# Last stage of a vision-tower kernel on one Trainium2 core: layer statistics in narrow matmuls, two broadcasts from a row, and a new table of places

## The chip, the cores and the metric

One NeuronCore of a Trainium2 chip runs the whole program in one launch. The metric is the device time of one execution in microseconds (us), the median of several; lower is better.

## The reference, cut to what matters

A tokenizer of two attention stages and a strided 3x3 unfold with a projection gives h: 4 images, 3136 tokens each, 768 channels, float32. The last stage of the kernel computes that projection and one layer on h:

```python
h = h + _L0_attn_ref(_layernorm(h), A, W_B, b_B, W_C, b_C, W_D, b_D, p_Delta)
h = h + _L0_ffn_ref(_layernorm(h), enc_w, enc_b, sw_w, sw_b, w1, b1, w2, b2)

def _ssm_forward(x, A, W_B, b_B, W_C, b_C, W_D, b_D, p_Delta):
    Bproj = x @ W_B + b_B                                   # 16 columns
    Cproj = x @ W_C + b_C
    delta = jax.nn.softplus(x @ W_D + b_D + p_Delta)        # W_D has one column
    dA = delta[..., None] * A
    A_bar = jnp.exp(dA)
    B_bar = (A_bar - A) / dA * delta[..., None] * Bproj[:, :, None, :]
    # h = a * h + b * x over the tokens, y = sum over the 16 states of c * h

# ffn: x_enc = x @ enc_w + enc_b (64 columns), 8 experts by argmax of a softmax,
#      gelu(x @ w1[e] + b1) @ w2[e] + b2, times the largest probability
```

## The kernel before

**Stages.** Two performer stages fill the first 3.1 ms or so and are not touched. The function `tail` is the last stage. It works in 28 units (4 images of 7 strips) of T = 448 tokens, channels on partitions in 6 chunks of 128. A unit has 24 steps (6 chunks by 4 groups of states); one step scans 4 x 448 columns.

**A step** on its engines: GpSimd (POOL) multiplies x by B into a ring of six buffers (`weigh_in`, L1604). ScalarE (ACT) writes four decays into PSUM (L1886), in two pairs, each as soon as VectorE has scanned that pair of the step before. VectorE (DVE) weighs each pair (L1995, two instructions) and scans it (L2004). ACT keeps the last states (`keep_states`, L1847). POOL multiplies by C (`weigh_out`, L1616), two steps behind its `weigh_in`. TensorE (PE) sums the states in four matmuls of 32 output rows (L1697) into PSUM bank 4 (YB); after four steps it adds h (L1701), and ACT copies the bank back to h (`add_to_h`, L1875).

**Other work** is put between the steps of unit i: `front(i + 1, k)` prepares the next unit (projection by six matmuls, "taps", a chunk, L1656 and L1658, and its copy to h, L1812; squares, L1804; sums, B, C, z and delta), and `mlp(i - 1, k)` finishes the last one (second layer norm, encoding, experts, routing, masks, output in eight blocks, L1759 to L1762). Each engine runs its program strictly in order, and the step k at which a piece stands on each engine is a constant of a table written by hand: P_ for PE, A_ for ACT, V_ for DVE.

```python
P_PJ, P_MU, P_VAR, P_Z, P_BC = 1, 7, (8, 10), 11, 9
A_HW, A_MU, A_SQ, A_RS, A_MX, A_SP = 5, 11, (9, 13), 14, (16, 17), (17, 18)
```

All this work shares the three PSUM banks BS, BX and BF (5, 6, 7): every tap goes to BF, so the tap of a chunk waits until ACT has copied the one before. Sums over the channels are matmuls with a 128 x 128 matrix of 1/768, whose answer stands in all 128 rows; W_D is repeated to 128 columns (`wz`) for the same reason.

**ACT's order in a step:** `add_to_h` where due, `start_states` (L1857), four decays, `keep_states` of the step before, then mlp and front. A wait in these stands ahead of the next decays. SyncE (SP) issues the loads, stores and spreads of x and delta through DRAM in program order too.

## Time and profile before

| | us |
|---|---|
| median of 3 runs (8669.71 to 8670.3) | 8670.22 |
| the profiled execution | 8669.5 |
| its span, first to last instruction | 8667.7 |
| PE busy | 7500.9 (87%) |
| DVE busy | 6217.8 (72%) |
| POOL busy | 5557.6 (64%) |
| ACT busy | 4309.3 (50%) |
| mean granted clock of PE | 0.916 |

The span is from the first instruction to the last. Busy shares are over the whole program; the last stage begins at about 3.1 ms, and what limits it is read from its own stretches. A matmul in float32 shows as two rows, so "x12" is six matmuls. Idle time is given in brackets with the instruction that ended it.

### The profile page before, as it was taken

Reading aid. Unit: us, or ns where it says so; the run is one execution under the profiler, and the core shown is the slowest. Engines: PE = TensorE matmul, PEld = TensorE weight load, DVE = VectorE, ACT = ScalarE, POOL = GpSimd, SP = SyncE. Lnnn points to the kernel's source line nnn. Section 1 sums busy time; section 2 is a strip of 40 time slices with the busy share of each in tenths; the row PEclk is TensorE's granted clock in tenths of the full one; section 3 lists DMA queues with packets and bytes.
Section 4 is the critical chain, followed back from the end, with each engine's and each line's share of the span. In section 5 each row is a group of like instructions: output and inputs, shape, how many; then the busy total and the mean of one; then the engine's idle time right before and its main releaser. Section 6 shows DMA issues by size and latency. Waiting matters only on the chain.

```text
span 8667.7 us, 87075 instructions
## 1 busy us (share of the span) xinstructions
PE 7500.9 (87%) x31228; PEld 3123.7 (36%) x31228; DVE 6217.8 (72%) x6601; ACT 4309.3 (50%) x7753; POOL 5557.6 (64%) x2486
## 2 busy tenths in 40 slices
PE   8999999979999856888888888878888888788877
PEld 6444444334444312333333333333333333333333
DVE  2566666822333339888888888888888888888884
ACT  3666666833444425455445444554444445544442
POOL 0111111267666319888888888888888888888884
PEclk9999999989999977988889999888989998899888
DMA  1111111145545222232333322323333233233321
GB/s 38 40 42 45 42 46 36 50 100 110 102 101 104 58 85 88 98 124 99 108 118 116 104 96 99 126 96 113 114 114 104 96 109 115 96 121 107 114 102 52
DMA packets 356921, 786.65 MB, mean 91 GB/s; under 512 B 70437, under 2 KB 282870, under 8 KB 349000
## 3 DMA queue, kind: packets, MB, share of 16 engines
q1 hardware_dynamic: 320440, 690.78, 26.3%
q0 software_dynamic: 21712, 51.75, 2.4%
q10 hardware_dynamic: 14336, 38.54, 1.2%
q8 instruction: 247, 4.05, 0.2%
q14 instruction: 186, 1.52, 0.1%
HBM read 597.39 MB, written 183.35 MB: 90 GB/s over the span
## 4 chain that ended last, share of the span: by engine, by line
PE 36%; DVE 16%; ACT 6%; issue 6%; POOL 0%; DMA 0%; SPq 0%; DVEq 0%; ACTq 0%; POOLq 0%
PE ps L1651 7%; DVE v L2004 7%; PE ps L1759 7%; DVE v L1995 6%; PE ps L1658 6%; PE ps L1656 6%; PE ps L1697 3%; ACT ps L1886 3%; PE ps L1647 2%; PE ps L1760 2%; PE ps L1762 2%; PE ps L1701 1%; DVE dl L1985 1%; DVE gm L2081 1%; ACT gm L1911 1%
## 5 line engine op out<-in xcount | busy, mean ns | idle before, releaser
L1616 POOL TENSOR_TENSOR v<-v,ct 128x1792 f32<-128x1792 f32 x672 | 2257.7, 3360 | 859.1 <-ACT st L1847 858.5
L2004 DVE TENSOR_TENSOR_SCAN v<-ps,v 128x901 f32<-128x901 f32 x1344 | 2732.2, 2033 | 92.2
L1886 ACT ACTIVATE ps<-dr,aa 128x448 f32<-128x448 f32 x2688 | 1586.0, 627 | 1526.2 <-DVE v L2004 1508.8
L1604 POOL TENSOR_TENSOR v<-xr,bt 128x1792 f32<-128x1792 f32 x672 | 2257.9, 3360 | 97.5 <-DMA xr<-h_by_channel 97.5
L1995 DVE SCALAR_TENSOR_TENSOR v<-ps,aa,v 128x448 f32<-128x448 f32 x2688 | 1689.1, 670 | 547.6 <-ACT ps L1886 528.9
L236 POOL DMA_DIRECT2D tokens<-ob x448 | 235.3, 532 | 1529.6 <-DVE ob L563 1486.7
L1759 PE MATMUL ps<-w_or_w,gm 128*112 128x384 f32 x1792 | 728.4, 556 | 370.7 <-DVE gm L2081 278.1
L1697 PE MATMUL ps<-v,dg 128*32 128x448 f32 x5376 | 702.6, 597 | 196.6 <-ACT h L1875 120.1
L1759 PEld LDWEIGHTS ps<-w_or_w,gm 128*112 128x112 f32 x1792 | 337.3, 199 | 772.1 <-DVE gm L2081 320.5
L1651 PE MATMUL ps<-h,w_or_w 128*128 128x448 f32 x1344 | 537.4, 550 | 17.7 <-DVE gm L2048 17.7
L1812 ACT ACTIVATE h<-ps,pbias 128x448 f32<-128x448 f32 x168 | 106.3, 633 | 721.9 <-PE ps L1658 721.9
L1656 PE MATMUL ps<-x,wpa 128*128 128x448 f32 x1008 | 445.9, 577 | 17.7 <-ACT h L1812 10.7
L1658 PE MATMUL ps<-x,wpb 64*128 64x448 f32 x1008 | 447.8, 575 | 0.0
L929 PE MATMUL ps<-xt,wa 128*64 128x448 f32 x2016 | 435.1, 565 | 0.0
L552 DVE COPY ht<-ps 112x512 f32<-112x512 f32 x112 | 77.4, 691 | 464.8 <-ACT kp L433 464.8
L1647 PE MATMUL ps<-sq,jm 128*128 128x448 f32 x672 | 317.3, 613 | 60.5 <-ACT ot L1920 56.5
L1651 PEld LDWEIGHTS ps<-h,w_or_w 128*128 128x128 f32 x1344 | 250.5, 191 | 300.5 <-issue 279.7
L586 DVE RECIPROCAL qpn<-qpn 128x448 f32<-128x448 f32 x112 | 330.7, 2953 | 3.9
L1697 PEld LDWEIGHTS ps<-v,dg 128*32 128x32 f32 x5376 | 110.1, 112 | 600.1 <-issue 292.1
L1746 PE MATMUL ps<-wpb 9*128 9x448 f32 x224 | 152.1, 769 | 194.7 <-DVE gm L2081 194.0
L1238 DVE TENSOR_TENSOR kq<-ps,rsa 128x896 f32<-128x896 f32 x56 | 61.1, 1092 | 358.6 <-PE ps L937 337.6
L1651 PE MATMUL ps<-h,wz 128*128 128x448 f32 x336 | 192.4, 742 | 100.9 <-ACT rs L1824 100.9
(324 smaller groups left out, 11785.1 us busy)
## 6 DMA issues: line engine op xcount, KB each, us to landing
xr<-h_by_channel SPq DMA_DIRECT2D x168, 896.0 KB, 7.5
dr<-delta_by_channel SPq DMA_DIRECT2D x168, 896.0 KB, 6.1
x<-tokens SPq DMA_DIRECT2D x252, 224.0 KB, 5.3
tokens<-ob POOLq DMA_DIRECT2D x448, 112.0 KB, 2.4
w_or_w<-in_w SPq DMA_DIRECT2D x29, 1536.0 KB, 6.4
w_or_w<-centred_w SPq DMA_DIRECT2D x27, 1536.0 KB, 6.4
h_by_channel<-h SPq DMA_DIRECT2D x112, 336.0 KB, 10.8
delta_by_channel<-dl SPq DMA_DIRECT2D x112, 336.0 KB, 5.1
```

The source lines that it names most:

```text
L929: mm(ps[half[g], o, 0:T], wa[:, j, cols], xt[:, 2 * (n % 3) + g, 0:TR2, j:j + 2 * S2 - 1:2], start=(j == 0), stop=False)
L1604: tt(v[:, n % RING, :, 2:T + 2], xr[:, dc % 2, :].rearrange("p (i t) -> p i t", i=4), bt[:, q:q + 1, :].to_broadcast([128, 4, T]), ALU.mul ...
L1616: tt(v[:, n % RING, :, 2:T + 2], v[:, n % RING, :, 2:T + 2], ct[:, q:q + 1, :].to_broadcast([128, 4, T]), ALU.mult).then_inc(s_cm, 1)
L1647: mm(into, jm[:, :], sq[:, dc % 3, :], start=(dc == 0), stop=(dc == DC - 1)).then_inc(s_var[ln], 1)
L1651: last = mm(into, weights(dc), h[:, i % 3, dc, :], start=(dc == 0), stop=(dc == DC - 1))
L1656: mm(into, even(j), x3[:, 0:TR3, j:j + 2 * S3 - 1:2], start=(j == 0), stop=False)
L1658: last = mm(into, odd(j), x3[0:64, 1:TR3 + 1, j:j + 2 * S3 - 1:2], start=False, stop=(j == 2))
L1697: last = mm(ps[32 * g:32 * g + 32, YB, 0:T], dg[:, 4 * k + g, :], v[:, n % RING, g, 2:T + 2], start=(q == 0), stop=False)
L1759: mm(into[:, 0:D // 2], gm[:, m, cs], w2[:, m, lo:lo + D // 2], start=(m == 0), stop=False)
L1886: fn(decay(g), dr[:, dc % 2, g, :], ACT.Exp, scale=aa[:, 4 * k + g:4 * k + g + 1]).then_inc(s_a, 1)
L1995: stt(row, decay(g), aa[:, 4 * k + g:4 * k + g + 1], row, ALU.subtract, ALU.mult).then_inc(s_wt, 1)
L2004: nc.vector.tensor_tensor_scan(row, flat[:, 1024 * pair + 1:1024 * pair + GW + T + 2], row, 0.0, ALU.mult, ALU.add).then_inc(s_sc, 1)
```

## The change

- **LN 1 (`sums_1`).** For each chunk three matmuls stand in a row: B, C and W_D together (49 output rows from partition 0), one tap of the token means (9 rows from 64) and the sum of squares (32 rows from 96), all into bank BS. Before, squares (128 rows, BF), B and C (48 rows, BS), means (BF) and W_D repeated (128 rows, BF) were four sets of six.
- **LN 2 (`sums_2`).** For each chunk the encoding (64 rows from 64), the mean (32 rows from 0) and the squares (32 rows from 32) go to bank BX.
- **z and deviation from a row.** z is scaled with C in one DVE instruction, and one matmul with `pick` spreads its row over 128 partitions. The second variance is subtracted in 32 rows and spread in the same way. The DVE scaling of z (L1970) is gone; ACT takes the logarithm of the first variance twice, in 32 rows each.
- **Banks.** The taps of chunks 0, 2, 5 go to BF, those of 1, 3, 4 to BS; the four expert products to BF, BF, BX, BS.
- **ACT** does its other work in half steps: `step` is cut in two pairs, work of place k stands between them and work of place k + 0.5 behind. `keep_states` now stands ahead of the second pair.
- **SP** stores and spreads delta in two halves, and four of its places move.
- **Places.** Nearly every constant of the table is new; TAIL is 29.

```diff
-        P_PJ, P_MU, P_VAR, P_Z, P_BC = 1, 7, (8, 10), 11, 9
-        A_HW, A_MU, A_SQ, A_RS, A_MX, A_SP = 5, 11, (9, 13), 14, (16, 17), (17, 18)
-        V_Z, V_BC, V_DL = 15, 14, (18, 19)
-        P_SQ, P_MEAN, P_ENC, P_IN, P_LOG, P_TURN = (0, 2), 1, 4, 5, 6, 10
-        P_MASK, P_OUT = (12, 13, 14, 15), (16, 17, 18, 18, 19, 20, 21, 22)
-        A_SQ2, A_MS, A_RS2, A_EX, A_GL = (2, 4), 5, 7, 11, 14
-        A_OUT = (21, 22, 23, 23, 24, 25, 26, 27)
-        V_VAR, V_ENC, V_IN, V_LOG, V_EQ, V_OH, V_MASK = 6, 8, 9, 10, 12, 14, (16, 17, 18, 19)
+        P_PJ, P_SUM, P_Z = (1, 3, 4, 5, 7, 8), (9, 11), 14
+        A_HW, A_SQ, A_MU, A_RS = (5, 6.5, 8, 9, 10.5, 12), (9.5, 12.5), 15, 14.5
+        A_MX, A_SP = (17, 17.5), ((18, 18.5), (19, 19.5))
+        V_BC, V_DL = 15, (18, 19)
+        P_SUM2, P_VAR, P_IN, P_LOG, P_TURN = (2, 4), 6, (10, 12, 13, 14), 8, 11
+        P_MASK, P_OUT = (15, 15, 17, 17), (18, 19, 20, 20, 21, 22, 23, 24)
+        A_SQ2, A_MS, A_RS2, A_EX, A_GL = (1, 5.5), 8, 9.5, 12, 17
+        A_OUT = (22, 22.5, 23.5, 24, 25, 26, 27, 28)
+        V_VAR, V_ENC, V_IN, V_LOG, V_EQ, V_OH, V_MASK = 7, 9, (12, 14, 15, 16), 11, 12, 13, (17, 17, 18, 18)
...
+            def sums_1(i, chunks):
+                for dc in chunks:
+                    pe.wait_ge(s_sq[0], DC * i + dc + 1)
+                    mm(ps[0:49, BS, 0:T], wbc[:, dc, :], h[:, i % 3, dc, :], start=(dc == 0), stop=(dc == DC - 1))
+                    tap(ps[few, BS, 0:T], lambda j: wma[:, j, :], lambda j: wmb[:, j, :], dc)
+                    mm(ps[top, BS, 0:T], jm[:, 0:32], sq[:, dc % 3, :], start=(dc == 0),
+                       stop=(dc == DC - 1)).then_inc(s_var[0], 1)
...
+                    if dc == 1:
+                        after(pe, s_oa, 2 * NCH * (i - 2))
+                        after(pe, s_bcs, 2 * i)
+                    if dc >= 2:
+                        pe.wait_ge(s_hw, DC * i + (dc - 1 if dc < 4 else 4))
...
+                if k == P_Z:
+                    pe.wait_ge(s_bcs, 2 * (i + 1))
...
+                    mm(bank(BF), pick[mid, 0, :], bcs[mid, :], start=True, stop=True).then_inc(s_z, 1)
...
+                    if m == 3:
+                        pe.wait_ge(s_bcs, 2 * min(i + 3, UNITS))
+                        pe.wait_ge(s_mu, min(i + 3, UNITS))
...
                     if i < UNITS:
                         start_states(i, k)
-                        step(i, k)
+                        step(i, k, 0)
+                    if i >= 1 and k == 2:
+                        add_to_h(i - 1, DC - 1)
+                    if i < UNITS and k >= 6 and k % 4 == 2:
+                        add_to_h(i, k // 4 - 1)
+                    others_due(i, k)
                     if i >= 1 and k == 0:
                         keep_states(i - 1, STEPS - 1)
                     elif i < UNITS and k > 0:
                         keep_states(i, k - 1)
...
+                    if i < UNITS:
+                        step(i, k, 1)
+                    others_due(i, k + 0.5)
```

**What it moves on the engines.** PE, steps 5 and 6 of a unit in the middle, before (dg is the sum of the states, w_or_w an expert product, wpa and wpb the taps):

```order
L1697 MATMUL ps<-v,dg 32x448 x4
L1651 MATMUL ps<-h,w_or_w 128x448 x6
L1656 MATMUL ps<-x,wpa 128x448 x3
L1658 MATMUL ps<-x,wpb 128x448 x3
L1697 MATMUL ps<-v,dg 32x448 x4
L1651 MATMUL ps<-h,w_or_w 128x448 x6
L1728 MATMUL ps<-wpb 112x8 x4
L1656 MATMUL ps<-x,wpa 128x448 x3
L1658 MATMUL ps<-x,wpb 128x448 x3
```

Now, PE's steps 5, 6 and the start of 7:

```order
L1734 MATMUL ps<-v,dg 32x448 x4
L1670 MATMUL ps<-x,wpa 128x448 x3
L1672 MATMUL ps<-x,wpb 128x448 x3
L1734 MATMUL ps<-v,dg 32x448 x4
L1749 MATMUL ps<-rs2t,pick 128x448
L1734 MATMUL ps<-v,dg 32x448 x4
L1738 MATMUL ps<-h,ident 128x448
L1670 MATMUL ps<-x,wpa 128x448 x3
L1672 MATMUL ps<-x,wpb 128x448 x3
```

The expert products have left these steps for 10 to 14, the next tap stands two steps on, and step 6 holds only the spread of the second variance.

PE, the sums of the first layer norm, before, from step 8 on:

```order
L1697 MATMUL ps<-v,dg 32x448 x4
L1651 MATMUL ps<-h,w_or_w 128x448 x6
L1647 MATMUL ps<-sq,jm 128x448 x3
L1697 MATMUL ps<-v,dg 32x448 x4
L1651 MATMUL ps<-h,wbc 48x448 x6
L1697 MATMUL ps<-v,dg 32x448 x4
L1733 MATMUL ps<-ident,eq 9x112 x4
L1647 MATMUL ps<-sq,jm 128x448 x3
L1697 MATMUL ps<-v,dg 32x448 x4
L1701 MATMUL ps<-h,ident 128x448
L1651 MATMUL ps<-h,wz 128x448 x6
```

Now, the start of step 9; the three narrow matmuls come three times here and three times in step 11:

```order
L1734 MATMUL ps<-v,dg 32x448 x4
L1679 MATMUL ps<-h,wbc 49x448
L1670 MATMUL ps<-x,wma 9x448
L1681 MATMUL ps<-sq,jm 32x448
L1679 MATMUL ps<-h,wbc 49x448
```

ACT, step 9 before (v<-st starts the states, ps<-dr,aa are decays, h<-ps,pbias is the copy of a tap):

```order
L1857 ACTIVATE v<-st 128x4
L1886 ACTIVATE ps<-dr,aa 128x448 x4
L1847 ACTIVATE st<-v 128x4
L1812 ACTIVATE h<-ps,pbias 128x448
L1804 ACTIVATE sq<-h 128x448 x3
```

Now, its step 9 with the half step behind it:

```order
L1899 ACTIVATE v<-st 128x4
L1928 ACTIVATE ps<-dr,aa 128x448 x2
L1852 ACTIVATE h<-ps,pbias 128x448
L1889 ACTIVATE st<-v 128x4
L1928 ACTIVATE ps<-dr,aa 128x448 x2
L1943 ACTIVATE rs2t<-ps,small 128x448
L1945 ACTIVATE rs2t<-rs2t 128x448
L1843 ACTIVATE sq<-h 128x448 x3
```

The copy of the tap and the kept states stand between the two pairs of decays; the statistics of the second layer norm and the squares stand behind the second pair.

## Rows read from the trace of the kernel before

**Rows 1.** Busy time by stretch: 20 units, units 1 to 26, unit 0, unit 27, the end
```profile
core 0: us, PE busy (x) PEld busy (x) DVE busy (x) ACT busy (x) POOL busy (x), PEclk, DMA share, GB/s
3967.50:7808.30 3840.80, 3234.19 (x11217) 1288.95 (x11216) 3357.50 (x3481) 1871.17 (x3980) 3199.75 (x961) 0.90 0.32 108
3395.50:8384.90 4989.40, 4189.11 (x14500) 1667.87 (x14496) 4364.65 (x4525) 2430.71 (x5170) 4159.99 (x1249) 0.89 0.32 108
3218.40:3395.50 177.10, 91.01 (x314) 27.66 (x314) 160.08 (x155) 82.32 (x175) 161.15 (x49) 0.71 0.34 115
8384.90:8562.30 177.40, 121.37 (x428) 46.90 (x424) 161.78 (x165) 76.46 (x172) 154.44 (x47) 0.76 0.19 72
8562.30:8667.70 105.40, 95.12 (x327) 45.63 (x326) 8.30 (x20) 16.72 (x30) 3.36 (x1) 0.95 0.15 50
```

**Rows 2.** Waits in the 20 units: us in total, times, longest us
```profile
DVE v L1995 <- ACT ps L1886: 402.0, 126, 4.8
DVE ps L1976 <- ACT rs L1826: 8.3, 20, 0.4
...
ACT h L1812 <- PE ps L1658: 527.5, 112, 7.5
ACT h L1875 <- PE ps L1701: 235.7, 80, 7.6
...
POOL v L1616 <- ACT st L1847: 640.5, 350, 5.3
```

**Rows 3.** Timeline of PE, steps 5 and 6 of unit 4: start, us
```profile
4029.79 0.96 PE L1697 MATMUL ps<-v,dg 128*32 128x448 f32 x8
4030.68 4.78 PE L1651 MATMUL ps<-h,w_or_w 128*128 128x448 f32 x12
4035.30 2.56 PE L1656 MATMUL ps<-x,wpa 128*128 128x448 f32 x6
4040.38 0.96 PE L1697 MATMUL ps<-v,dg 128*32 128x448 f32 x8
```

**Rows 4.** Timeline of ACT and DVE, the same place
```profile
4036.43 2.03 DVE L2004 TENSOR_TENSOR_SCAN v<-ps,v 128x901 f32<-128x901 f32 x1
...
4040.49 0.63 ACT L1812 ACTIVATE h<-ps,pbias 128x448 f32<-128x448 f32 x1 [7.53 <-PE ps L1658]
...
4043.79 1.27 DVE L1995 SCALAR_TENSOR_TENSOR v<-ps,aa,v 128x448 f32<-128x448 f32 x2 [4.81 <-ACT ps L1886]
```

**Rows 5.** Timeline of PE in the second performer stage
```profile
2502.06 0.96 PE L932 MATMUL ps<-x,wc 128*64 128x448 f32 x4
2502.86 2.55 PE L929 MATMUL ps<-xt,wa 128*64 128x448 f32 x12
2505.24 0.96 PE L932 MATMUL ps<-x,wc 128*64 128x448 f32 x4
2506.14 1.02 PE L937 MATMUL ps<-x,wc 64*64 64x448 f32 x8
```

**Rows 6.** Groups of ACT and DVE in the 20 units: busy us, mean ns
```profile
L1970 DVE TENSOR_TENSOR ps<-ps,rs 128x448 f32<-128x448 f32 x20 | 12.1, 606 | 0.0
...
L1832 ACT ACTIVATE dl<-ps,pc 128x448 f32<-128x448 f32 x120 | 66.4, 620 | 0.0
...
L1911 ACT ACTIVATE gm<-gm,b 128x448 f32<-128x448 f32 x80 | 47.0, 657 | 0.2
L1911 ACT ACT_TABLE_LOAD x20 | 25.7, 1283 | 0.4
```

**Rows 7.** Timeline of PE after a wait in unit 14
```profile
6010.42 7.57 PE L1651 MATMUL ps<-h,wz 128*128 128x448 f32 x12 [3.83 <-ACT rs L1824]
```

**Rows 8.** Timeline, from the first tap to the first decays
```profile
3142.13 4.18 PE L1656 MATMUL ps<-x,wpa 128*128 128x448 f32 x6 [6.99 <-DVE w_or_w L2114]
...
3198.84 4.78 PE L1651 MATMUL ps<-h,wz 128*128 128x448 f32 x12 [0.72 <-ACT rs L1824]
...
3214.96 3.76 SPq L1488 DMA_DIRECT2D delta_by_channel<-dl  x4
...
3229.94 2.31 ACT L1886 ACTIVATE ps<-dr,aa 128x448 f32<-128x448 f32 x4 [16.87 <-DMA dr<-delta_by_channel]
```

**Rows 9.** Timeline of PE behind the last scan
```profile
8583.06 2.52 PE L1647 MATMUL ps<-sq,jm 128*128 128x448 f32 x6 [1.01 <-ACT ot L1920]
...
8596.93 4.78 PE L1651 MATMUL ps<-h,w_or_w 128*128 128x448 f32 x12
```

**Rows 10.** DMA issues in the 20 units: KB each, median us to landing
```profile
xr<-h_by_channel SPq DMA_DIRECT2D x120, 896.0 KB, 7.6
...
w_or_w<-in_w SPq DMA_DIRECT2D x20, 1536.0 KB, 6.4
```

More of the change, by code:

```diff
@@ L1555, in _ @@
                 spread_c(0, q)
-            store_delta(0)
-            spread(0, 0)
+            spread_x(0, 0)
+            store_delta(0, 0)
+            spread_delta(0, 0)
+            store_delta(0, 1)
             for i in range(UNITS):
@@ L1642, in _ @@
             mm = nc.tensor.matmul
-            def squares_sum(i, ln, into, chunks):
-                for dc in chunks:
-                    pe.wait_ge(s_sq[ln], DC * i + dc + 1)
-                    mm(into, jm[:, :], sq[:, dc % 3, :], start=(dc == 0), stop=(dc == DC - 1)).then_inc(s_var[ln], 1)
             def over_chunks(into, weights, i):
@@ L1652, in over_chunks, with tap, sums_2 @@
                 return last
-            def taps(into, even, odd):
-                for j in range(3):
+            def tap(into, even, odd, j):
+                if j < 3:
                     mm(into, even(j), x3[:, 0:TR3, j:j + 2 * S3 - 1:2], start=(j == 0), stop=False)
-                for j in range(3):
-                    last = mm(into, odd(j), x3[0:64, 1:TR3 + 1, j:j + 2 * S3 - 1:2], start=False, stop=(j == 2))
-                last.then_inc(s_pj, 1)
+                else:
+                    return mm(into, odd(j - 3), x3[0:64, 1:TR3 + 1, j - 3:j - 4 + 2 * S3:2], start=False,
+                              stop=(j == 5))
+            def sums_1(i, chunks):
[5 more added lines that the diff above has]
+                       stop=(dc == DC - 1)).then_inc(s_var[0], 1)
+            def sums_2(i, chunks):
+                for dc in chunks:
+                    pe.wait_ge(s_sq[1], DC * i + dc + 1)
+                    mm(ps[up, BX, 0:T], enc[:, dc, :], h[:, i % 3, dc, :], start=(dc == 0), stop=(dc == DC - 1))
+                    mm(ps[low, BX, 0:T], jm[:, 0:32], h[:, i % 3, dc, :], start=(dc == 0), stop=(dc == DC - 1))
+                    mm(ps[mid, BX, 0:T], jm[:, 0:32], sq[:, dc % 3, :], start=(dc == 0),
+                       stop=(dc == DC - 1)).then_inc(s_var[1], 1)
             def front(i, k):
-                if P_PJ <= k < P_PJ + DC:
-                    dc = k - P_PJ
+                for dc in range(DC):
+                    if P_PJ[dc] != k:
+                        continue
                     cols = slice(128 * dc, 128 * dc + 128)
@@ L1820, in front @@
                     squares(i, 0, range(3, DC))
+                if k == A_MU:
+                    act.wait_ge(s_var[0], DC * (i + 1))
+                    fn(means(i), ps[few, BS, 0:T], ACT.Identity, bias=mub[few, :]).then_inc(s_mu, 1)
                 if k == A_RS:
@@ L1875, in add_to_h, with step @@
                 fn(h[:, i % 3, dc, :], bank(YB), ACT.Copy).then_inc(s_hy, 1)
-            def step(i, k):
+            def step(i, k, pair):
                 dc, q = divmod(k, Q)
                 n = STEPS * i + k
-                if q == 0:
+                if q == 0 and pair == 0:
                     act.wait_ge(s_dr[dc % 2], 16 * ((DC // 2) * i + dc // 2 + 1))
-                for g in range(4):
-                    if g % 2 == 0 and n > 0:
-                        free_pair(n - 1, g // 2)
+                if n > 0:
+                    free_pair(n - 1, pair)
+                for g in range(2 * pair, 2 * pair + 2):
                     fn(decay(g), dr[:, dc % 2, g, :], ACT.Exp,
@@ L1925, in mlp, with others_due @@
                         act.dma_start(dst, ot[:, ch % 2, :]).then_inc(s_out[ch % 2], 16)
+            def others_due(i, k):
+                if i >= 2 and k + STEPS < TAIL:
+                    mlp(i - 2, k + STEPS)
+                if i >= 1:
+                    mlp(i - 1, k)
+                if i + 1 < UNITS:
+                    front(i + 1, k)
             act.sem_inc(s_in, 1)
```

245 lines of the change are left out of this document (118 added, 127 removed).

## The prediction

> **What bounds the kernel now.** I read the busy time by stretch first. Twenty units of the last stage take 3840.8 us, 192.0 each; DVE is busy for 167.9 of a unit, PE for 161.7, POOL for 160.0 [rows 1]. Three engines stand near 85% and none is full, so the waits come next. In these 20 units DVE waits 402.0 us for ACT's decays and 8.3 for the deviation, 20.5 a unit, and for nothing else that is listed [rows 2]. ACT is not slow (1871 of 3841 us busy [rows 1]): it stands 527.5 us before its copies of the taps and 235.7 before its copies of h, both times for PE, and its program is in order, so the next decays stand behind that copy. POOL waits only for the states that ACT keeps, 640.5 us [rows 2]. The timeline shows one case: PE's step 5 holds the sum of the states, an expert product and a tap and takes from 4029.79 to 4040.38, 10.6 us [rows 3]. ACT waits 7.53 us for this tap, and DVE, whose last scan began at 4036.43, gets its decays at 4043.79, 4.81 us late [rows 4]. A mean step of DVE without its waits is (192.0 - 20.5) / 24 = 7.15 us. So PE binds the kernel in the steps where taps and other products stand together, and DVE elsewhere.
>
> From rows 3, each start taken to the next: the sum of the states costs 0.89 us, six matmuls of a set 4.62 (0.77 each), a tap set 5.08 (0.85 each). I write Tk for the end of DVE's step k. PE can begin step k when POOL has weighed it, some 3.7 us behind Tk (3.36 of POOL and a kept state).
>
> **PE's load.** Removed are 36 matmuls of sets of six (12 squares, W_D, B and C, mean, encoding) and 6 taps of the means: 36 x 0.77 + 6 x 0.85 = 32.8 us a unit. Added are 12 groups of three and two spreads (2 x 0.77 = 1.5). The trace holds no group of unlike widths. The lower end is the group of four equal 32-row matmuls, 0.89, which gives 10.7; the upper is every matmul for itself with a break before it. The nearest row for the break: four rows of 128x64 followed by the same shape start 0.80 us before it, followed by 64x64 they start 0.90 before it [rows 5], so 0.10 a change, and 36 x 0.87 = 31.3. I take the value between: only equal shapes run together, which are the means with the squares in three groups and the two 32-row sums in six, so 9 x 2 + 3 x 3 = 27 turns of 0.87, 23.5 us, because the only change of shape in the rows does show a break. PE then has 161.7 - 32.8 + 23.5 + 1.5 = 153.9 us a unit (141.1 at the lower end).
>
> The Trainium skill speaks against the change here: "TensorEngine Tiling (Array Packing)", Tiling Modes, says that changing the tiling mode, not just the tile, drains TensorE. The break in rows 5 agrees in kind; no row shows unlike shapes side by side. By that rule the groups cost the 23.5 us of the sum, and without it 10.7.
>
> **Where PE's work stands.** Before, its steps 1 to 8 held eight states (7.1), six tap sets and that of the means (7 x 5.1), the squares of both norms by halves (4.6), mean, encoding and four experts (27.7) and 2.6 of small work: 77.7 us, 9.7 a step against 7.15. Now steps 1 to 8 hold eight states, six taps, six groups (10.4), a spread and the same small work: about 51 us, 6.4 a step. The heaviest are 4 (0.9 + 5.2 + 5.1 = 11.2) and 11 (10.5, odd taps), each with a light neighbour. The experts stand in 10, 12, 13, 14, with 5.5 each.
>
> Then the copies, step by step. A tap's copy on ACT, between the pairs of step k, comes about 2 us before T(k-1). Tap 0 (PE 1) ends at T2 + 3.5 and is copied near T4 - 2, 8 us of slack; tap 4 (PE 7) ends near T8 + 4.4 and its copy at 10.5 is due at T9 + 1.4, 4 us; tap 5 (PE 8), behind a wait for the encoding at T9 + 0.7, ends near T10 and is due near T11 - 2. The second bank is what lets PE run ahead. Copies of h moved one step earlier, from 7 to between the pairs of 6; PE's output blocks moved from two in 18 to two in 20, so that the block of h in step 19 no longer stands behind them. The 20.5 us of DVE's waiting go, and 0.6 of the removed scaling of z (L1970) [rows 6]: 192.0 - 20.5 - 0.6 = 170.9 us a unit, the floor.
>
> **What comes in its place.** (a) Expert 1 (PE 12) stands behind the long step 11, whose turn of the routing waits for DVE until T12 + 2, and ends at about T14: DVE waits 0.8 us. (b) Expert 3 (PE 14) now waits for B and C, which DVE writes 2.6 us behind T15. PE idles some 3.5 us there. After 3.83 us of idling a set took 7.57 instead of 4.78 us [rows 7]; with the same surcharge the product ends 1 us behind T16, 1.0 us of DVE. Behind this wait on PE stand the spread of z and the states of step 15; both are wanted later. (c) ACT's place 17 holds between the pairs two table loads, four gelus and three copies of z, 2 x 1.28 + 4 x 0.66 + 3 x 0.62 = 7.1 us [rows 6], while from its start to the moment DVE wants the second pair there are about 4.8 us: 2.3 us. Together 4.1, so **175.0 us a unit**. The two logarithms of 32 rows, the copy of the means and the deviation lie in ACT's idle time, which is half of it; if a wait falls into the same half step they cost their own 0.6 us. `keep_states` now stands ahead of the second pair, delays it by 0.2 us of 2 us of slack and serves POOL a microsecond earlier. DVE's narrow operations keep their durations.
>
> SP: the w2 load waits for expert 3 (PE 14, about T16), and behind it in the queue stands the spread of x for the last chunk, which POOL wants near T17 + 4. The load takes 6.4 us and a spread 7.6 to land [rows 10], so POOL may idle up to 4 us; it has 175.0 - 160.0 = 15 us to spare, so it costs nothing here (a rival below). Delta's two stores give the next unit's first spread some 5 us earlier; it had slack.
>
> **The ends.** Units 1 to 26 took 4989.4 us [rows 1], now 26 x 175.0 = 4550.0: 439.4 saved. Unit 0 saves the 0.6 of z. Unit 27 has no front: 177.4 us with DVE busy 161.8 [rows 1]; with the same 3.6 us of small gaps as a full unit (171.5 - 167.9) and 1.3 of waits it is 166.7, 10.7 saved. From the first tap to the first decays 87.8 us pass [rows 8]. There each removed set of six is on the path; 18 squares, B and C and W_D plus the means' taps (19.0) become 13.8 of groups and one spread, the taps no longer wait for each copy (5 x 0.7), and delta is stored in halves: about 15 (10 to 22). Behind the last scan the squares, the mean and the encoding take 13.9 us on PE (8583.06 to 8596.93) [rows 9] and become 10.4, output blocks lag by less, a longer chain to the first expert costs some back: 8 (3 to 12).
>
> **Sum.** 439.4 + 0.6 + 10.7 + 15 + 8 = 473.7. Against the profiled execution's 8669.5 us that is **8196 us**; the median of the runs is 0.7 above it, which changes nothing.
>
> **The rivals.**
> 1. *PE still binds part of the unit.* At 153.9 us of 175 it is as full as before (84% then, 88% now) and has four waits of its own (encoding, routing, B and C, output copies). If each of the turns cost the upper 31.3 us instead of 23.5, PE needs 162 us; with the waits a unit is about 182: 8669.5 - 26 x 9.9 - 34 = 8378. For it: no row shows unlike shapes together. Against it: the load is spread evenly.
> 2. *POOL starves behind the w2 load.* The late spread of x and states kept behind ACT's longer middle part take POOL's reserve; a unit of 178 gives 8669.5 - 26 x 13.9 - 34 = 8274.
> 3. *The clock falls, and the kernel becomes slower.* PE's granted clock is 0.90 with PE busy 84% of the time, 0.76 with 68% (unit 27) and 0.71 with 51% (unit 0) [rows 1]. The sets at the prices of rows 3 add up to 142 us a unit at full speed. If the thinned work left the clock at 0.70, PE would need 142 / 0.70 = 203 us, 11 more than now: 8669.5 + 26 x 11 - 34 = 8922. It decides from 142 / 192 = 0.74 down. Against it: PE stays above 80% busy, between the first two stretches, so I expect 0.87 or more. "TensorE: Matmul & The Clock Gate", Part 1, of the Trainium skill holds that half rate is the default and that activity releases it, which is this rival's rule; the three stretches agree with it in direction.
> 4. *The change doesn't do what it says.* ACT's waits on PE are only hidden waits on something else in the ring, and DVE loses the same 20 us behind another releaser: within 0.2%, about 8660.
>
> **Chances.** The forecast 0.64 (own range 8090 to 8250: with the lower price of the groups and no new waits 171 us a unit, 8092; with 177, 8248), rival 1 0.16, rival 2 0.12, rival 3 0.04, rival 4 0.04. A measurement tells about 0.2%, 17 us, from no change. Faster by more 0.92, within 0.04, slower 0.04. The range of 8 in 10 runs from 8090 to 8380 and takes in rivals 1 and 2.
>
> **What would show it.** A full unit of 175 us, with DVE above 95% busy; DVE's wait for decays under 5 us a unit instead of 20.1, and most of it at the gelus; ACT's waits for taps and h nearly gone (38 us a unit now); POOL at about 92%; PE 150 us or less a unit and its clock not under 0.85. In the groups, starts of the three matmuls within 0.02 us of each other would mean 0.89 a group; 0.4 us apart would mean turns. I am wrong if DVE still waits over 10 us a unit, if its waits name POOL's `v`, or if the granted clock of a unit is under 0.8.

## The result and the profile after

| | us |
|---|---|
| median of 4 runs (8262.34 to 8265.36) | 8263.43 |
| kernel before, same chip (8669.5 to 8670.3) | 8669.97 |
| ratio, 95% interval | 0.9531 [0.9515, 0.9548] |
| the profiled execution | 8263.1 |
| its span, first to last instruction | 8261.3 |
| mean granted clock of PE | 0.918 |

The changed kernel takes 4.7% less time. The profiled executions differ by 406.4 us; 473.7 were predicted. Busy time by stretch in the changed kernel; the stretches are unit 0, units 1 to 26, the same 20 units as in [rows 1], unit 27, and the end behind the last scan:

```profile
core 0: us, PE busy (x) PEld busy (x) DVE busy (x) ACT busy (x) POOL busy (x), PEclk, DMA share, GB/s
3208.00:3385.10 177.10, 88.51 (x304) 23.21 (x304) 159.44 (x154) 82.97 (x176) 162.16 (x49) 0.68 0.36 117
3385.10:7988.40 4603.30, 4030.82 (x14295) 1492.07 (x14296) 4354.56 (x4499) 2456.79 (x5197) 4149.57 (x1249) 0.90 0.36 117
3915.10:7457.50 3542.40, 3107.15 (x11036) 1151.68 (x11034) 3349.69 (x3461) 1890.84 (x4000) 3192.01 (x961) 0.90 0.36 117
7988.40:8156.80 168.40, 118.60 (x437) 42.80 (x436) 161.73 (x164) 77.01 (x171) 153.55 (x47) 0.78 0.21 76
8156.80:8261.30 104.50, 91.92 (x314) 42.89 (x312) 8.29 (x20) 16.82 (x30) 3.35 (x1) 0.92 0.15 50
```

Against [rows 1], units 1 to 26 gained 4989.4 - 4603.3 = 386.1 us, unit 27 9.0, the end 0.9 and the time up to unit 0 10.4 (it begins at 3208.0 instead of 3218.4); unit 0 gained nothing. That is the whole 406.4. A full unit takes 3542.4 / 20 = 177.1 us instead of 192.0, with DVE busy 94.6% of it. PE's busy time fell by 6.3 us a unit (161.7 to 155.4) while the unit fell by 14.9.

The waits in the 20 units (us in total, times, longest), of DVE and the longest of ACT:

```profile
DVE gm L2121 <- PE ps L1785: 51.1, 40, 2.0
DVE v L2038 <- ACT ps L1928: 39.7, 20, 2.0
DVE gm L2090 <- PE ps L1665: 24.7, 37, 1.2
...
ACT ps L1928 <- DVE v L2047: 935.7, 400, 6.3
```

L1928 are the decays, L2038 and L2047 DVE's weighing and scan, L1665 an expert product, L1785 an expert's mask, L2121 DVE's product with it, L2090 DVE's scaling of an expert product. DVE's 402.0 us behind the decays [rows 2] are 39.7, one wait a unit. ACT no longer waits for PE before its copies of taps or of h at all; PE holds it for 23.2 us before the first variance, and otherwise it waits for DVE. New are 51.1 us before the masks, 2.6 a unit, and 24.7 before the scaling of expert products, 1.2 a unit.

What makes DVE wait there can be followed in the timeline of unit 14 (start and duration in us, in brackets the idle time before and its releaser). ACT, its place 17 (L1952 the gelus, L1873 the copies of z, L1889 the kept state):

```profile
5804.63 1.28 ACT L1952 ACT_TABLE_LOAD   x1
5805.93 2.35 ACT L1952 ACTIVATE gm<-gm,b 128x448 f32<-128x448 f32 x4
5808.29 1.28 ACT L1953 ACT_TABLE_LOAD   x1
5809.59 1.68 ACT L1873 ACTIVATE dl<-ps,pc 128x448 f32<-128x448 f32 x3
5811.15 0.21 ACT L1889 ACTIVATE st<-v 128x4 f32<-128x4 f32 x1
```

POOL's weighing of the finished states, PE's sum of the states (L1734) and masks, and DVE:

```profile
5811.44 3.36 POOL L1634 TENSOR_TENSOR v<-v,ct 128x1792 f32<-128x1792 f32 x1 [6.97 <-ACT st L1889]
...
5815.74 1.72 PE L1734 MATMUL ps<-v,dg 128*32 128x448 f32 x8 [4.79 <-ACT h L1917]
5821.50 1.72 PE L1734 MATMUL ps<-v,dg 128*32 128x448 f32 x8 [4.03 <-POOL v L1634]
5823.15 3.35 PE L1785 MATMUL ps<-wpb 9*128 9x448 f32 x4
...
5812.48 1.28 DVE L2038 SCALAR_TENSOR_TENSOR v<-ps,aa,v 128x448 f32<-128x448 f32 x2 [2.03 <-ACT ps L1928]
5825.12 0.62 DVE L2121 TENSOR_TENSOR gm<-gm,ps 128x448 f32<-128x448 f32 x1 [1.69 <-PE ps L1785]
```

One block of ACT makes both waits. Its second pair of decays comes 2.03 us late, and the states of step 16, which it keeps just ahead of that pair, come so late that POOL stands 6.97 us. From there POOL works without a gap and is through with step 17 at 5821.44 only. PE's sum of that step waits for it until 5821.50; behind it stand two masks, and after the idle time sum and masks take twice as long as in steps without a wait, the level of 1.2 instead of 2.4 GHz: 1.72 us for the sum instead of 0.96, and 3.35 for the masks instead of the 1.76 of the two at 5809.19. The granted clock of that stretch, 5821.5 to 5826.5, is 0.50. With 0.89 for the sum and 0.88 for each mask both would have been there at about 5824.2, and DVE was free at 5823.43: an estimate of some 0.2 us of waiting instead of 2.56. So the late states cost that much because the idle time that they make is also followed by the lower level.

### The profile page after: what moved, and what is told of

Same layout as the page of the kernel before. It is cut to its first block, busy times and chain, and to the rows that moved or that the text cites. A ratio compares the mean times of both kernels' runs of the same rounds, so it can differ in the third digit from the quotient of the medians.

```text
span 8261.3 us, 86870 instructions
## 1 busy us (share of the span) xinstructions
PE 7327.8 (89%) x31004; PEld 2931.6 (35%) x31004; DVE 6205.4 (75%) x6573; ACT 4337.3 (53%) x7781; POOL 5547.7 (67%) x2487
## 4 chain that ended last, share of the span: by engine, by line
DVE 28%; PE 15%; issue 11%; POOL 4%; ACT 4%; DMA 0%; DVEq 0%; SPq 0%; ACTq 0%; POOLq 0%
DVE v L2038 13%; DVE v L2047 13%; PE ps L1665 3%; POOL v L1634 3%; PE ps L1670 2%; PE ps L1672 2%; PE ps L1734 2%; PE ps L1679 2%; POOL v L1622 1%; DVE dl L2028 1%; PE ps L1681 1%; PE ps L1785 1%; ACT ps L1928 1%; ACT gm L1952 1%; PE ps L1798 0%
## 5 line engine op out<-in xcount | busy, mean ns | idle before, releaser
L2047 DVE TENSOR_TENSOR_SCAN v<-ps,v 128x901 f32<-128x901 f32 x1344 | 2732.1, 2033 | 95.0 <-DVE v L2038 2.7
L1928 ACT ACTIVATE ps<-dr,aa 128x448 f32<-128x448 f32 x2688 | 1595.9, 626 | 1319.6 <-DVE v L2047 1303.2
L2038 DVE SCALAR_TENSOR_TENSOR v<-ps,aa,v 128x448 f32<-128x448 f32 x2688 | 1687.5, 669 | 71.5 <-ACT ps L1928 67.9
L1734 PE MATMUL ps<-v,dg 128*32 128x448 f32 x5376 | 792.3, 632 | 616.2 <-POOL v L1634 395.1
L1798 PE MATMUL ps<-w_or_w,gm 128*112 128x384 f32 x1792 | 694.4, 535 | 3.0 <-DMA w_or_w<-in_w 3.0
L1665 PE MATMUL ps<-h,w_or_w 128*128 128x448 f32 x1344 | 588.7, 592 | 84.9 <-DVE bcs L2022 84.9
L1889 ACT ACTIVATE st<-v 128x4 f32<-128x4 f32 x672 | 140.9, 210 | 893.5 <-DVE v L2047 893.5
L1670 PE MATMUL ps<-x,wpa 128*128 128x448 f32 x1008 | 497.1, 632 | 7.6 <-DVE w_or_w L2154 6.9
L1734 PEld LDWEIGHTS ps<-v,dg 128*32 128x32 f32 x5376 | 126.3, 114 | 1026.3 <-POOL v L1634 550.2
L1672 PE MATMUL ps<-x,wpb 64*128 64x448 f32 x1008 | 452.2, 580 | 0.0
L1665 PEld LDWEIGHTS ps<-h,w_or_w 128*128 128x128 f32 x1344 | 268.4, 206 | 408.3 <-issue 302.6
L1670 PEld LDWEIGHTS ps<-x,wpa 128*128 128x128 f32 x1008 | 202.0, 210 | 260.3 <-issue 257.8
L290 PE MATMUL ps<-wki,h 128*112 128x256 f32 x896 | 275.9, 389 | 1.9 <-DVE hu L544 1.9
L1672 PEld LDWEIGHTS ps<-x,wpb 64*128 64x128 f32 x1008 | 175.8, 187 | 275.1 <-issue 275.1
```

The costliest lines, as they stand in the source:

```text
L1665: last = mm(into, weights(dc), h[:, i % 3, dc, :], start=(dc == 0), stop=(dc == DC - 1))
L1670: mm(into, even(j), x3[:, 0:TR3, j:j + 2 * S3 - 1:2], start=(j == 0), stop=False)
L1672: return mm(into, odd(j - 3), x3[0:64, 1:TR3 + 1, j - 3:j - 4 + 2 * S3:2], start=False, stop=(j == 5))
L1734: last = mm(ps[32 * g:32 * g + 32, YB, 0:T], dg[:, 4 * k + g, :], v[:, n % RING, g, 2:T + 2], start=(q == 0), stop=False)
L1798: mm(into[:, 0:D // 2], gm[:, m, cs], w2[:, m, lo:lo + D // 2], start=(m == 0), stop=False)
L1928: fn(decay(g), dr[:, dc % 2, g, :], ACT.Exp, scale=aa[:, 4 * k + g:4 * k + g + 1]).then_inc(s_a, 1)
```

## The experiments

All but the three that say so go from the changed kernel. They ran on chips on which the kernel before takes 8677 to 8678 us; by its ratio the changed kernel would take 0.9531 x 8678 = 8271 there (an estimate), and it is the ratios that are compared. A unit is the mean over 20 full units of the profiled execution.

### The masks, the copies of z, and both

```diff
-        P_MASK, P_OUT = (15, 15, 17, 17), (18, 19, 20, 20, 21, 22, 23, 24)
+        P_MASK, P_OUT = (15, 15, 16, 16), (18, 19, 20, 20, 21, 22, 23, 24)
```

> Edit to the changed kernel: the third and fourth mask product of the experts move from PE's step 17 to its step 16, so they no longer stand behind the sum of the states of step 17, which POOL weighs late because ACT's block at place 17 keeps the states late. Theory A (place 17 is the cause of the masks' wait): DVE's 2.6 us a unit on the masks (L2121) go, a unit 177.1 becomes 174.5, time about 8263 - 27 x 2.6 = 8195. Rival B (the wait moves on: the next thing that is late is DVE's decays in the same step, so DVE waits the same time at L2038): a unit stays within 0.5 us of 177.1, time 8250 to 8263.

```diff
-        A_MX, A_SP = (17, 17.5), ((18, 18.5), (19, 19.5))
+        A_MX, A_SP = (17.5, 18), ((18, 18.5), (19, 19.5))
```

> Edit to the changed kernel: ACT's three capped copies of z (first half) move from the middle of place 17, where they stand behind the four gelus and two table loads, to half a step later, and the second half from there to 18. Theory A: the block before the second decay pair of step 17 shrinks from 7.1 to about 5.2 us, DVE's wait for decays (2.0 us a unit) goes, states are kept 1.9 us earlier and the masks' wait falls too: a unit 173 to 175, 8155 to 8215. Rival B (ACT's block isn't what ends last; the gelus must wait for DVE's last product anyway, and the copies of z now delay the first pair of step 18): DVE waits 2 us at another decay, a unit stays at 177, 8255 to 8270.

> Both edits (masks in PE's step 16, copies of z half a step later). If the two waits are separate costs, 2.6 + 2.0 us a unit go: a unit 172.5, 8263 - 27 x 4.6 = 8139. If both come from the one block of place 17, this gives no more than the better of the two single edits (about 8195).

Masks alone: 8184.91 us, ratio 0.9433 [0.942, 0.9446], a unit 174.0. Copies alone: 8243.26, 0.95 [0.9487, 0.9513], a unit 176.3. Both: 8144.18, 0.9386 [0.9374, 0.9399], a unit 172.5. DVE's waits in 20 units, for the three in this order:

```profile
DVE v L2038 <- ACT ps L1928: 40.5, 20, 2.0
DVE gm L2090 <- PE ps L1665: 17.1, 28, 0.8
```
```profile
DVE gm L2121 <- PE ps L1785: 66.3, 40, 2.8
...
DVE v L2038 <- ACT ps L1928: 8.1, 18, 0.5
```
```profile
DVE gm L2090 <- PE ps L1665: 19.1, 29, 1.2
DVE v L2038 <- ACT ps L1928: 8.1, 18, 0.5
```

With the masks in step 16 the wait for them is gone and nothing takes its place; the unit falls by 3.1 us, 0.5 more than that wait, of which 0.4 is a shorter wait at the experts. With the copies moved, the wait for decays falls from 2.0 to 0.4 us a unit, but the masks' wait grows from 2.6 to 3.3, so that only 0.8 of the 1.6 us reach the unit: that part of theory A fell. The reason is the next block. ACT's place 18 now holds the second three copies and the exponential, and keeps the states of step 17 behind them, so that POOL waits for just these. Its row in that run:

```profile
5811.67 3.36 POOL L1634 TENSOR_TENSOR v<-v,ct 128x1792 f32<-128x1792 f32 x1 [0.73 <-ACT st L1889]
```

Together the two edits give what the two waits promise, 4.6 us a unit. By ratio that is 0.0145, a little more than 0.0098 and 0.0031 of the single ones. The rival, that with one block behind both waits the two edits give no more than the better one, fell: the block is one, but it reaches DVE by two paths, and each edit opens one of them. This version beats both kernels and computes the same outputs.

### PE's load: the kernel before with less of it

These three go from the kernel before, and leave all places as they were.

```diff
-                    over_chunks(bank(BX), lambda dc: jm[:, :], i).then_inc(s_mean, 1)
+                    over_chunks(bank(BX), lambda dc: jm[:, :], i, DC - 1).then_inc(s_mean, 1)
...
```

> Edit to the kernel before: the mean, the product of W_D, that of B and C, and the encoding use one matmul instead of six each (the sixth chunk alone; five sixths of each sum are left out), 20 matmuls less, 15.4 us of PE a unit (161.7 to 146), everything in its old place. Theory L (load): PE has as much room as in the changed kernel, and the 20.5 us of waits for decays go: a unit under 177, about 8280 or less. Theory P (places): most of the wait stays, because in steps 1 to 6 ACT still wants each tap in the step in which PE makes it; the lighter steps are 4 (mean and encoding) and 9 to 11. A unit of 182 to 188, 8400 to 8570.

The next took the same number of matmuls from other steps, and the one after it took both (both edits in one kernel):

```diff
-                    over_chunks(bank(BS), lambda dc: w1[:, dc, 128 * m:128 * m + 128], i).then_inc(s_hm, 1)
+                    over_chunks(bank(BS), lambda dc: w1[:, dc, 128 * m:128 * m + 128], i, DC - 1).then_inc(s_hm, 1)
```

> Edit to the kernel before: each of the four expert products in PE's steps 5 to 8 uses one matmul instead of six (the sixth chunk alone; five sixths of each product are left out): 20 matmuls less, as many as in the run that thinned the mean, W_D, B and C and the encoding, which brought a unit from 192.0 to 187.7 us. Theory S (what counts is PE's load in the steps where one bank passes from tap to copy to tap: steps 5 and 6 hold a tap and an expert each, and step 7 the means' taps and an expert): the waits for decays of DVE's steps 9 to 12, 13.6 us a unit, go, and the wait of step 23 stays: a unit of 178 to 180, about 8300 to 8370. Theory L (any 15 us less of PE count the same): 187 to 188 a unit, about 8545.

> Edit to the kernel before: both cuts together, 40 matmuls less (five sixths of the mean, W_D, B and C, encoding and expert sums are left out), PE's load some 31 us a unit lower, all places as before. Theory S: the waits of steps 3, 9 to 12 go, and 4 us of step 23 stay, where ACT's copy of h stands behind two output products on PE: a unit of 176 to 178, 8260 to 8320. Rival (ACT's order alone makes part of the waits, whatever PE does): 182 or more, 8400 or above.

| | ratio to before | unit, us | PE busy a unit |
|---|---|---|---|
| kernel before | 1 | 192.0 | 161.7 |
| thin sums | 0.9846 [0.9833, 0.986] | 187.7 | 149.9 |
| thin experts | 0.9743 [0.9728, 0.9757] | 184.4 | 149.8 |
| both | 0.9732 [0.9717, 0.9746] | 184.4 | 138.5 |
| the change | 0.9531 [0.9515, 0.9548] | 177.1 | 155.4 |

This is the main finding, and none of the theories had it whole. The thin sums met theory P (182 to 188 us a unit), the thin experts fell between S and L, and both cuts together met the number of the rival, 182 or more. The place of the load counts: 20 matmuls out of the steps 5 to 8 give 7.6 us a unit, 20 out of others 4.3. But with 40 out and PE 17 us less busy than in the changed kernel, the unit is still 7.3 us longer than there. DVE still waits 12.6 us a unit for decays (20.1 before):

```profile
DVE v L1995 <- ACT ps L1886: 252.6, 60, 7.5
```

They stand at two places. One is in the middle of the unit, 6.9 us of the 12.6 (137.7 in 20 units), and its cause is new. PE's waits for DVE's scaling of an expert product show what came up. They add up to 45.0 us with thin sums and 98.8 with thin experts; the rows of the kernel before and of both cuts, in 20 units:

```profile
PE ps L1651 <- DVE gm L2048: 11.1, 20, 0.6
```
```profile
PE ps L1651 <- DVE gm L2048: 171.4, 51, 5.5
```

The timeline of the run with both cuts: PE's step 6, then ACT, then DVE there and at the second place:

```profile
4017.87 1.86 PE L1651 MATMUL ps<-h,w_or_w 128*128 128x448 f32 x2 [5.45 <-DVE gm L2048]
...
4021.26 4.85 PE L1656 MATMUL ps<-x,wpa 128*128 128x448 f32 x6
4026.03 3.26 PE L1658 MATMUL ps<-x,wpb 64*128 64x448 f32 x6
...
4029.33 0.63 ACT L1812 ACTIVATE h<-ps,pbias 128x448 f32<-128x448 f32 x1 [10.67 <-PE ps L1658]
...
4033.00 1.28 DVE L1995 SCALAR_TENSOR_TENSOR v<-ps,aa,v 128x448 f32<-128x448 f32 x2 [7.54 <-ACT ps L1886]
...
4126.83 1.28 DVE L1995 SCALAR_TENSOR_TENSOR v<-ps,aa,v 128x448 f32<-128x448 f32 x2 [3.75 <-ACT ps L1886]
```

All four expert products of the kernel before go through bank BS, so the second one must wait until DVE has read the first, which DVE does in its step 9. Behind that wait on PE stands the tap of the same step, behind the tap ACT's copies of it and of a chunk of h, behind the copies the decays. After idling, the tap takes 8.0 us (4021.26 to 4029.23, granted clock 0.62) instead of 5.1 to 5.2. It is a ring: DVE waits for decays, which wait for a tap, which waits for DVE. In the kernel before PE was so late that the wait was 0.6 us a unit and looked harmless; the load hid it. The changed kernel has the experts in steps 10 and 12 to 14, where no tap of a full set stands, and in three banks.

The second place lies about the turn of the unit and holds the other 5.7 us (115.0 in 20 units; 100.9 in the kernel before, so that the cuts took nothing from it). There ACT waits 6.73 us, until 4125.00, to copy h, and PE reaches the last product of that copy only behind two output blocks in one step (4114.39 to 4123.06); the expectation of this run had named that wait, with 4 us. The change moves these copies and blocks too, and both waits are gone from its trace. Its 7.3 us against the run with both cuts are these 12.6 less its own new waits. How much belongs to the experts' steps, to their banks, and to the copies and output blocks is not shown: none of these moves was run alone.

### PE's load: the changed kernel with more of it

```diff
-                    mm(ps[0:49, BS, 0:T], wbc[:, dc, :], h[:, i % 3, dc, :], start=(dc == 0), stop=(dc == DC - 1))
+                    mm(ps[0:49, BS, 0:T], wbc[:, dc, :], h[:, i % 3, dc, :], start=(dc == 0), stop=False)
+                    mm(ps[0:49, BS, 0:T], wbc[:, dc, :], h[:, i % 3, dc, :], start=False, stop=(dc == DC - 1))
...
```

> Edit to the changed kernel: in each of the 12 groups the first matmul (B and C; encoding) is issued twice, 12 more turns of about 0.87 us, 10.4 us of PE a unit, which puts PE's busy time at 166 us a unit, above the 161.7 of the kernel before; B, C, z and the encoding come out doubled. Nothing else moves. Theory L (the load of PE was what bound the kernel before, and its fall is the gain): DVE waits again for decays behind late taps, a unit of 187 us or more, 8520 or above. Theory P (the places are the gain: no copy of ACT is due right behind the set that it needs, and the second bank lets PE run ahead): a unit of 177 to 180, 8265 to 8340.

8377.29 us, ratio 0.9654 [0.9641, 0.9668], a unit 180.9: between the theories. A repeated matmul costs 0.77 to 0.79 us, 9.4 a unit, so PE's load, busy for 160.6 us a unit at a clock of 0.92, is near that of before, and still the unit is 11.1 us shorter than before. DVE's waits for decays (39.7 us in 20 units) and masks (51.0) are unchanged; ACT waits for taps again, 99.5 us, and none of it reaches DVE. 3.7 of the 3.8 us stand at the expert products, nearly all at experts 0 and 1, where the change had 24.7 in all:

```profile
DVE gm L2092 <- PE ps L1665: 99.2, 42, 2.9
```

So load still counts in the changed kernel, in the steps 9 to 14 with groups and experts, and no longer in those with the taps.

### The taps in a row

```diff
-        P_PJ, P_SUM, P_Z = (1, 3, 4, 5, 7, 8), (9, 11), 14
-        A_HW, A_SQ, A_MU, A_RS = (5, 6.5, 8, 9, 10.5, 12), (9.5, 12.5), 15, 14.5
+        P_PJ, P_SUM, P_Z = (1, 2, 3, 4, 5, 8), (9, 11), 14
+        A_HW, A_SQ, A_MU, A_RS = (5, 6, 7, 8, 9, 12), (9.5, 12.5), 15, 14.5
```

> Edit to the changed kernel: the first five taps go back to one each in PE's steps 1 to 5 and ACT's copies to the middle of 5 to 9 (the sixth stays in 8 and 12); the squares' groups, experts and everything else stay. Each fourth step then holds a tap and a group of three or both. Theory (the spread of the taps over eight steps and the two banks are needed): ACT waits for taps again, some 3 to 8 us of them reach DVE, a unit of 180 to 185, 8340 to 8480. Rival (with the sums thinned to 5 us and the experts moved away, steps 1 to 6 are light enough in any order): a unit within 1 us of 177.1, 8240 to 8290.

8276.44 us, ratio 0.9537 [0.9521, 0.9553], which cannot be told from the change (0.9531); a unit 177.7. The rival was right. ACT does wait again for taps, but for 5.2 us a unit, in two waits of at most 3.6, and they are hidden: DVE has the first pair by then. The 0.5 us of the unit stand at the first expert (10.2 us in 20 units before the edit, 20.3 now). The two banks of the taps stay as they are in this run.

```profile
ACT h L1852 <- PE ps L1672: 103.8, 40, 3.6
```

### Half steps, and where the states are kept

```diff
                         step(i, k, 0)
+                        step(i, k, 1)
...
-                    others_due(i, k)
...
-                    if i < UNITS:
-                        step(i, k, 1)
+                    others_due(i, k)
```

> Edit to the changed kernel: ACT issues both pairs of decays of a step one behind the other, and only then the copy of h, the kept states and the other work, as the kernel before did for its other work; the places stay the same but for the half steps. Theory A (half steps matter: the work between the pairs is hidden behind the scan of the first pair, and the states reach POOL a microsecond earlier): later states make POOL and PE's sums late, and blocks of 5 us ahead of a first pair reach DVE: a unit of 180 to 184, 8340 to 8440. Rival B (half steps are only a finer table): within 0.2% of 8263. The opposite is possible too: the block of place 17 then has a whole step ahead of it, and the wait of 2.0 us goes.

> Edit to the changed kernel: ACT keeps a step's states behind the second pair of decays, as the kernel before did, instead of ahead of it; that gives them to POOL about 1.3 us later. Theory A (states kept late are what makes the masks wait): in step 17 POOL begins 1.3 us later, the masks' wait grows from 2.6 to about 3.9 us a unit and nothing else changes: 8263 + 27 x 1.3 = 8298. Rival (the second pair is what is late in step 17, and keeping states behind it gives DVE 0.2 us): 8255 to 8265.

Whole steps: 8355.62 us, 0.9629 [0.9616, 0.9642], a unit 180.1; theory A at its lower end. Two of DVE's waits in 20 units:

```profile
DVE v L2037 <- ACT ps L1928: 50.8, 20, 2.8
DVE rs2t L2078 <- ACT rs2t L1940: 39.0, 20, 2.0
```

With those for the masks (57.9) and the experts (28.5) they add up to 8.8 us a unit against 5.8 before the edit, which is the 3.0 of the unit. Two thirds of it is a wait that is new: ACT's square of the mean (L1940) comes behind both pairs instead of between them. The decays are the smaller part.

States kept behind the pair: 8280.3 us, 0.9543 [0.9528, 0.9557], which overlaps the change; a unit 177.5. The masks' wait grew from 51.1 to 75.1 us in 20 units, 1.2 a unit as theory A has it, so the late states are what the masks wait for. But the wait at the experts (L2090) fell from 24.7 to 11.6, and only 0.4 us a unit was lost.

### Equal shapes in the groups

```diff
-                    mm(ps[0:49, BS, 0:T], wbc[:, dc, :], h[:, i % 3, dc, :], start=(dc == 0), stop=(dc == DC - 1))
+                    for rows in (low, zr):
+                        mm(ps[rows, BS, 0:T], wbc[:, dc, rows], h[:, i % 3, dc, :], start=(dc == 0),
+                           stop=(dc == DC - 1))
...
```

> Edit to the changed kernel: in the groups every matmul gets the shape 128 rows by 32 columns (B and C's weights in two halves, the encoding's in two halves, the odd rows of the means' taps padded with zeros to 128), so that four equal shapes stand side by side on the four column groups. The same sums are computed. Theory A (matmuls run together only if their shapes are equal): a group takes 0.9 us instead of 1.77 or 2.65, PE's busy time falls by some 13 us a unit (155.4 to 142); the rival (each set of columns takes turns whatever its shape, because the data stream is different) makes a group four turns, 3.5 us, and PE 171. For the time: if PE's load no longer binds the full unit, theory A changes a unit by at most 1.2 us (the experts' wait) and saves 5 to 12 us at the start and end: 8220 to 8260. If the load still binds, a unit falls by 3 us or more: under 8180.

> Equal shapes in the groups, the masks in PE's step 16 and the copies of z half a step later, together; the same outputs. If the three are independent: a unit of about 172, start 8 us shorter, end 5 us shorter, 8263 - 27 x 4.6 - 13 = 8126. If PE's thinner load lowers its granted clock (0.90 in a full unit), the long sets behind idle stretches eat part of it: 8150 to 8200.

The first: 8263.74 us, 0.9522 [0.9509, 0.9535], not to be told from the change. Two groups in the changed kernel (L1679 B, C and W_D, L1670 or L1672 a tap of the means, L1681 the squares), an even tap and an odd one:

```profile
5763.24 0.95 PE L1679 MATMUL ps<-h,wbc 128*49 128x448 f32 x2
5764.12 0.57 PE L1670 MATMUL ps<-x,wma 128*9 128x448 f32 x1
5764.13 0.94 PE L1681 MATMUL ps<-sq,jm 128*32 128x448 f32 x2
...
5765.03 0.95 PE L1679 MATMUL ps<-h,wbc 128*49 128x448 f32 x2
...
5776.80 0.95 PE L1679 MATMUL ps<-h,wbc 128*49 128x448 f32 x2
5777.68 0.96 PE L1672 MATMUL ps<-x,wmb 64*9 64x448 f32 x2
5778.57 0.94 PE L1681 MATMUL ps<-sq,jm 128*32 128x448 f32 x2
5779.44 0.95 PE L1679 MATMUL ps<-h,wbc 128*49 128x448 f32 x2
```

And with the edit, "equal shapes":

```profile
5763.31 0.54 PE L1680 MATMUL ps<-h,wbc 128*32 128x448 f32 x2
5763.33 0.58 PE L1670 MATMUL ps<-x,wma 128*9 128x448 f32 x1
5763.33 0.54 PE L1687 MATMUL ps<-sq,jm 128*32 128x448 f32 x1
...
5764.06 0.55 PE L1680 MATMUL ps<-h,wbc 128*32 128x448 f32 x2
```

A group takes 1.79 us, 2.64 us, and 0.75 us. Theory A holds for the price, though its shapes are not equal: the four matmuls have 128 rows and 32, 17, 9 and 32 columns. What runs together here has 128 rows and at most 32 columns; the 49 columns and the 64 rows of the changed kernel take turns of their own. PE's busy time fell from 155.4 to 145.5 us a unit. The rule of the Trainium skill, "TensorEngine Tiling (Array Packing)", Tiling Modes, that a change of the tiling mode drains TensorE, agrees with the turns in the first two. Yet the unit is 177.4, none of it gained. PE's granted clock fell with its load, from 0.90 to 0.86. These are the groups of expert products (us in total, mean ns of one row, idle before them) in 20 units of the change and of this run:

```profile
L1665 PE MATMUL ps<-h,w_or_w 128*128 128x448 f32 x960 | 418.2, 590 | 65.0 <-DVE bcs L2022 65.0
```
```profile
L1665 PE MATMUL ps<-h,w_or_w 128*128 128x448 f32 x960 | 470.3, 649 | 156.4 <-DVE bcs L2030 98.0 <-ACT h L1860 58.4
```

PE comes to its waits earlier, idles 4.6 us more a unit, and the products behind them run at a lower clock; DVE's wait for them went from 24.7 to 36.2 us. By product: the wait at expert 1 (12.2 us) is gone, as theory A has it, but that at expert 0 went from 10.2 to 17.4 and that at expert 3 from 2.3 to 18.7. The set of expert 3 now stands behind 4.90 us of idle time instead of 3.25 and takes 7.4 to 7.8 us in 17 of the 20 units, where it took 6.47 in 16. With all three edits the time is 8143.81, 0.9383 [0.937, 0.9396], the same as without the equal shapes (0.9386): a unit that is 0.4 us longer gives back 11 us, and the start and the end, where PE works alone, bring some 6 and 5. By ratio that is 0.9383 x 8670 = 8135 us, between the 8126 of independent parts and the 8150 to 8200 of a lower clock.

## Why the prediction was right, and where it was off

**What bounded the kernel** was named rightly as the wait for decays behind ACT's waits for PE, and its 20.5 us a unit went to 2.0. The floor of 170.9 us holds: 177.1 less the 5.9 us of DVE's remaining waits is 171.2. Nothing else released DVE those 20 us late, so rival 4 fell. But the reading that PE's load in the steps with taps was the cause is half of it: 40 matmuls less in the old places (31 us at 0.77 each; PE is busy for 23 us less, at a clock of 0.82) bring 7.7 of the 14.9 us, because the ring through the one bank of the experts comes up behind them and the wait for the copies of h stays. The prediction credited PE's freedom to run ahead to the taps' spread and second bank; with the taps in a row the time cannot be told from the change, so the spread was not needed. The second bank was not tried alone.

**PE's load.** 27 turns, 23.5 us, were forecast by the reading that only equal shapes run together, with 9 and 32 columns taken as equal; the groups take 1.77 us for LN 2 and 1.79 and 2.64 for LN 1, which is 6 x 1.77 + 3 x 1.79 + 3 x 2.64 = 23.9. PE's busy time is 155.4 against 153.9 of the sum. The later sentence, that the profile would show 150 or less, contradicted the sum and was wrong.

**New waits: 4.1 us a unit forecast, 5.9 measured.** This is the step that failed, and 26 x 1.8 = 47 us of the 67 that are missing. (c), the block of place 17, was 2.3 and is 2.0. (a), expert 1, was 0.8 and is 0.6. (b), expert 3, was 1.0 and is 0.1: PE idles 3.25 us before it as forecast, but the set behind took 6.47 us in 16 of the 20 units, not 7.57, and DVE waits only in the two in which it took 7.75. Expert 0, which the prediction put at nothing, costs 0.5. What was left out is the masks' 2.6: the forecast followed the block of place 17 to DVE's second pair and stopped. That states kept late cost POOL its reserve stood in rival 2, but the forecast set POOL's 15 us of spare time in a unit against it and put the cost at nothing. Spare time over the unit does not help in the one step: the forecast did not go from POOL to PE's sum of step 17, and from there to what stands behind that sum on PE. It credited `keep_states` ahead of the pair with serving POOL a microsecond earlier; that is so (the masks' wait grows by 1.2 us a unit without it), but the same place puts the states behind everything else between the pairs, in step 17 behind 6.5 us of it (5804.63 to 5811.15).

**The ends.** The start was to gain 15 us and gained 10.4; the end 8, and gained 0.9. One reason is common to both. PE in the changed kernel behind the last group, first at the start (L1721 the spread of z), then at the end (L1749 the deviation, L1768 the logits, L1665 expert products):

```profile
3193.32 1.60 PE L1721 MATMUL ps<-bcs,pick 32*128 32x448 f32 x2 [4.05 <-DVE bcs L2022]
...
8186.37 1.01 PE L1749 MATMUL ps<-rs2t,pick 32*128 32x448 f32 x2 [1.28 <-DVE rs2t L2079]
8189.38 1.66 PE L1768 MATMUL ps<-wpb 64*112 64x8 f32 x8 [2.00 <-DVE wpb L2083]
8190.96 6.33 PE L1665 MATMUL ps<-h,w_or_w 128*128 128x448 f32 x12
...
8220.13 5.14 PE L1798 MATMUL ps<-w_or_w,gm 128*112 128x384 f32 x8 [2.97 <-DMA w_or_w<-in_w]
```

The groups end sooner, as forecast (8184.9 is 28.1 us behind the last scan; before, the sums ended 34.6 behind it), but now the logarithm, the exponential and the product on DVE stand between the last group and the spread, where the long product of W_D or the encoding used to cover them. At the start that chain shows as 4.05 us of idle time and a spread of 1.60: from the end of the last sums to ACT's first copy of z 5.7 us pass, 6.3 before. There two other terms were off as well: the taps gained 7.0 us instead of 3.5 (40.6 before, 33.6 now), and the two halves of delta 0.5 where the sum left some 6 for them (from ACT's first copy of z to the first decays 25.6 us before, 25.1 now). At the end it moves the first expert from 8184.9 to 8190.96, and 6 of the 6.5 us are gone. "A longer chain to the first expert costs some back" named it and did not count it. Then the first output block waits 2.97 us for w2, and the first expert product, which stood behind no idle time before, takes 6.33 us instead of 4.78.

**Unit 27** gained 9.0 for 10.7: DVE waits 3.1 us in it, 2.6 of them for the masks, where 1.3 were allowed. Unit 0 gained nothing for 0.6: DVE's first work begins 13.3 us into it, 12.9 before.

**The number and its luck.** 8263 lies outside the forecast's own range, 8090 to 8250, and inside the wide one. It is next to the 8274 of rival 2, and a unit of 177.1 next to its 178, which is luck in the number, as half of the rival's mechanism did not occur.

**Rivals.** Rival 2: POOL has no wait for a DMA in the 20 units, only for kept states (350.4 us), so the w2 load starved nobody, and DVE never waits for POOL. Its other half, the states kept behind ACT's longer middle part, is what the masks wait for. Rival 3: the clock of a full unit stayed at 0.90. Its mechanism is seen elsewhere, though: in the run with equal shapes the clock fell to 0.86, and slower sets took back what the shorter groups gave. Rival 1 at 182 us a unit was near what the doubled matmuls gave (180.9), by the experts' path and not by the taps.
